# Routed rows added into three tables in memory, and the last shared products left in PSUM

## The chip, the cores and the metric

The kernel runs on one core of a Trainium2 chip. The metric is the device time of one execution in microseconds (us). All inputs and outputs are float32; the matrix products of the feed-forward part split each float32 operand into a high and a low part and sum three products.

## The reference, cut to what matters

```python
x = layernorm(x + attention(x))              # x: (2, 1024, 256), causal, 16 query heads, 4 key heads of 16
# feed-forward: one shared expert for every token, and 4 of 16 routed experts per token
scores = sigmoid(x @ gate_w.T) + gate_b
weights, indices = top_k(scores, 4);  weights /= weights.sum(-1)
shared = (silu(x @ w1_s) * (x @ w3_s)) @ w2_s                     # hidden width 176
routed = sum over the 4 chosen e of weights[e] * (silu((x @ w1[e]) * (x @ w3[e])) @ w2[e])
x = layernorm(x + shared + routed)
```

## The kernel before

The 2048 tokens are 16 tiles of 128 tokens. The span falls into three stages.

**Attention** (to about 310 us) follows one order written out by hand (`ORDER`, `plan`, `SEQ`), which every engine walks; an engine does its own part of each item. The DMA queue of SyncE (SP) walks it too: key and query parts, mask rows (`mrow`, one per group of heads, 16 of them) and weight loads. `padrow` is a row of zeros with a marker; SP writes it behind the expert regions of `xs_scratch`. At the end of each half of a batch the tokens are routed, and GpSimd (POOL) scatters each token's row, with its expert numbers, weights and four destinations, into the regions of its four experts (`scatter_rows`, 64 indirect DMAs).

**Feed-forward** runs 48 pairs of tiles (`NPAIR`): 4 shared pairs (`EARLY`, tiles 0 to 7), 40 routed pairs (`NRP`; the last of them, `LASTR` = pair 43, has one tile, so there are 79 routed tiles, `MOST`), then 4 shared pairs (44 to 47, tiles 8 to 15). Per pair TensorE (PE) turns the rows (`rows_back`), multiplies up into `psH` (`up`), turns the gated result (`gated_back`) and multiplies down into `psY` (`down`), interleaved over neighbouring pairs. A down product waits until `psY` of the pair before has been read. For a routed pair n (of 40), ScalarE (ACT) scales `psY` into `ys` (two buffers, `NYS`), and POOL scatters each tile of `ys` to `y4_scratch` (`send`, L839): every token has four rows of its own there, one per choice, so no two writes meet; rows of padding are out of bounds and dropped. For a shared pair VectorE (DVE) adds half of `psY` to the rows in `x1` (`scaled`, L1363). The last group of tokens is routed during the first pairs (`LATE`), and POOL's last eight row scatters stand one behind each of the first eight sends. SP loads the rows of routed pair n into `xs` three pairs ahead (L697 to L699).

**The end**: once the last up product is done and all sends have landed, SP reads `y4_scratch` back, four rows per token, 16 DMAs of 512 KB (L709). For each of the 16 tiles the four rows and the row of `x1` are summed: 8 tiles on PE (`token_rows`, L1739 and L1741: products with the identity into a PSUM bank, 5 rows of 256 columns), 6 on POOL (L854, L855, L858), 2 on DVE (L1371 to L1373); `ADDER` says who. Then come mean and variance on DVE (`statistics`), a square root on ACT (`deviation`), the reciprocal and shift on DVE (`shifts`), the scaling on ACT (`normalised`) and the output DMA (L713), in the units of `UNITS` and the order of `LAST_ORDER`.

Of the kernel before, what the change touches and what calls it, by code (L numbers as in the profile page):

```python
# [66 lines left out]
ADDER = (("pool", "dve"), ("pe", "pool"), ("pe", "pool"), ("pe", "pool"), ("pe", "pool"), ("pe", "pool"), ("pe", "dve"), ("pe", "pe"))  # L67
GATHER = [2, 1, 0] + list(range(3, NT))
SUMS = [(n, t) for n in range(NSHP) for t in range(2) if ADDER[n][t] == "pe"]
POOLED = [(n, t) for n in range(NSHP) for t in range(2) if ADDER[n][t] == "pool"]  # L70
UNITS = [((n, 0), (n, 1)) for n in range(NSHP - 1)] + [((NSHP - 1, t),) for t in range(2)]
LAST_ORDER = [("stat", 0), ("stat", 1), ("shift", 0), ("stat", 2), ("shift", 1), ("stat", 3), ("shift", 2), ("stat", 4), ("shift", 3),
              ("sum", 6, 1), ("shift", 4), ("stat", 5), ("stat", 6), ("shift", 5), ("stat", 7), ("shift", 6), ("shift", 7), ("stat", 8),
              ("shift", 8)]
FAR = B * T * TOPK
NXS, NYS, NSEL = 3, 2, 6
NSCAT = 8
PAD0 = 5
# [115 lines left out]
LASTU = [("wU", s) for s in range(10, NX)]  # L194

# [47 lines left out]
CONSTS, MASKS = 16, 10  # L243
# [10 lines left out]
def attention_moe(nc, x, wq_w, wq_b, wk_w, wk_b, wv_w, wv_b, cp_w, cp_b, gate_w, gate_b,  # L254
# [3 lines left out]
    y4_dram = nc.dram_tensor("y4_scratch", (FAR, C), F32, kind="Internal").ap()  # L258

    ctx = ExitStack()  # L260
    with ctx:
# [35 lines left out]
        j128 = sb("j128", [P, 1])  # L297
        lg = sb("lg", [P, TH, NE])
# [67 lines left out]
        y4 = sb("y4", [P, NT, TOPK, C])  # L366
# [120 lines left out]
        s_ysc = [sem(f"s_ysc{i}") for i in range(NYS)]  # L487
        s_y4a = [sem(f"s_y4a_{i}") for i in range(NSHP)]
        s_y4b = [sem(f"s_y4b_{i}") for i in range(NSHP)]
# [29 lines left out]
        def sum_bank(n, t):  # L519

            c = slice(0, C) if t else slice(C, 2 * C)
            if (n, t) == (NSHP - 1, 1):
                return psR[:, c]
            return (psR[:, c], psR2[:, c], psX[:, 1 - t, :, :].rearrange("p k t -> p (k t)"),
                    psG[:, 1 - t, :, :].rearrange("p k t -> p (k t)"), psH[:, 0, c], psH[:, 1, c], psY[:, 0, c], psY[:, 1, c])[n]
# [14 lines left out]
        def _(sp):  # L540
# [80 lines left out]
            def run(item):  # L621
# [24 lines left out]
                elif kind == "mrow":  # L646

                    k = item[1]
                    sp.wait_ge(s_Tfree, T_NO[item])
                    g = HEADGROUPS[k][2]  # L650
                    sp.dma_start(QS[ROWS:QROWS, QAT[(k // 2) % NSLOT], g % 2 * G:(g % 2 + 1) * G, :]
                                 .rearrange("s h (i t) -> s (h i) t", t=P), MT[:, :]).then_inc(s_mrow, 16)
                elif kind == "wload":
                    freed(item[1:])
                    load_weights(item[1:])

# [24 lines left out]
            for n in range(NRP):  # L681
# [23 lines left out]
            for i in range(NYS):  # L705
                sp.wait_ge(s_ysc[i], 16 * len([n for n in range(MOST) if n // 2 % NYS == i]))
            y4_rows = y4_dram.rearrange("(i p k) c -> p i (k c)", p=P, k=TOPK)
            for i in GATHER:
                sp.dma_start(y4[:, i, :, :].rearrange("p k c -> p (k c)"), y4_rows[:, i, :]).then_inc((s_y4a, s_y4b)[i % 2][i // 2], 16)  # L709
            for unit in UNITS:  # L710
                i0, i1 = 2 * unit[0][0] + unit[0][1], 2 * unit[-1][0] + unit[-1][1] + 1
                sp.wait_ge(s_norm2, i1)
# [5 lines left out]
        def _(pool):  # L718
# [30 lines left out]
            nc.gpsimd.iota(x1row[:, :, DT], pattern=[[P * TOPK, NT], [1, TOPK]], base=-FAR, channel_multiplier=TOPK,  # L749
# [82 lines left out]
            def send(n):  # L832

                pool.wait_ge(s_sel, n + 1)
                for t, s in enumerate((s_y0, s_y1)):
                    if 2 * n + t == MOST:
# [13 lines left out]
            def token_rows(n, t):  # L850

                i = 2 * n + t
                pool.wait_ge((s_y4a, s_y4b)[t][n], 16)
                link(nc.gpsimd.tensor_tensor(y4[:, i, 0:2, :], y4[:, i, 0:2, :], y4[:, i, 2:4, :], ALU.add))  # L854
                link(nc.gpsimd.tensor_tensor(y4[:, i, 0, :], y4[:, i, 0, :], y4[:, i, 1, :], ALU.add))  # L855
                if n >= EARLY:
                    pool.wait_ge((s_y0, s_y1)[t], n + NRP + 1)
                nc.gpsimd.tensor_tensor(x1[:, i, :], x1[:, i, :], y4[:, i, 0, :], ALU.add).then_inc(s_added, 1)  # L858

            pool.wait_ge(s_g, NPAIR)  # L860
            for n, t in POOLED:
# [4 lines left out]
        def _(act):  # L866
# [162 lines left out]
            def scaled(m):  # L1029
# [6 lines left out]
                if n >= NYS:  # L1036

                    act.wait_ge(s_ysc[n % NYS], 32 * (n // NYS))
# [34 lines left out]
            def normalised(u):  # L1073

                act.wait_ge(s_shift, u + 1)
                for n, t in UNITS[u]:
                    row = x1[:, 2 * n + t, :]
                    nc.scalar.activation(row, sum_bank(n, t) if (n, t) in SUMS else row, ACT.Identity, scale=rs2[:, n, t:t + 1],
                                         bias=sh2[:, n, t:t + 1]).then_inc(s_norm2, 1)

            act.wait_ge(s_const, CONSTS)
            for step in LAST_ORDER:
# [7 lines left out]
        def _(dve):  # L1090
# [217 lines left out]
            def product(m):  # L1308
# [4 lines left out]
                nc.vector.tensor_tensor(z[:, :, :], h1[:, :, :], psH[:, :, HID:2 * HID], ALU.mult).then_inc(s_z, 1)  # L1313
# [20 lines left out]
            def match(n):  # L1334
# [3 lines left out]
                if n >= NSEL:  # L1338
                    dve.wait_ge(s_y0, EARLY + n - NSEL + 1)
                    dve.wait_ge(s_y1, EARLY + n - NSEL + 1)  # L1340
                    dve.wait_ge(s_ysc[n % NYS], 32 * ((n - NSEL) // NYS + 1))
# [8 lines left out]
                nc.vector.tensor_scalar(dst[:, j, :], sel[:, j, :, 1], float(FAR), None, ALU.add).then_inc(s_sel, 1)  # L1350

            def scaled(m):

                if not shared(m):
# [3 lines left out]
                if n == 0 or n >= EARLY:  # L1358
                    for h in range(GROUPS - 1 if n == 0 else GROUPS):
# [6 lines left out]
            def token_rows(n, t):  # L1366

                i = 2 * n + t
                row = x1[:, i, :]
                dve.wait_ge((s_y4a, s_y4b)[t][n], 16)  # L1370
                link(nc.vector.tensor_tensor(y4[:, i, 0:2, :], y4[:, i, 0:2, :], y4[:, i, 2:4, :], ALU.add))  # L1371
                link(nc.vector.tensor_tensor(y4[:, i, 0, :], y4[:, i, 0, :], y4[:, i, 1, :], ALU.add))
                link(nc.vector.tensor_tensor(row, row, y4[:, i, 0, :], ALU.add))  # L1373

            for i in range(-2, NPAIR + 2):
                if 0 <= i < NPAIR:
                    gated(i)
                if i - 2 == NPAIR - 1:
                    token_rows(0, 1)
# [10 lines left out]
                for item in late(i, 0):  # L1390
                    run(item)
                if 0 <= i < NPAIR:
# [5 lines left out]

            def statistics(u):

                for n, t in UNITS[u]:
                    row = x1[:, 2 * n + t, :]
                    if ADDER[n][t] == "pe":
                        dve.wait_ge(s_sum, max(SUMS.index(u_) for u_ in SUMS if u_[0] == n and (n < NSHP - 1 or u_ == (n, t))) + 1)
# [410 lines left out]
```

## Time and profile before

| | us |
|---|---|
| median of 3 runs (547.24 to 548.96) | 547.45 |
| the profiled execution | 546.37 |
| its span, first to last instruction | 544.6 |
| PE busy | 519.8 (95%) |
| DVE busy | 431.9 (79%) |
| ACT busy | 372.5 (68%) |
| POOL busy | 290.4 (53%) |

Durations and starts below are from the one profiled execution and count from the start of its span; some 1.8 us of its time lie outside the span. Busy time of a DMA queue is not shown; a DMA has a time from issue to landing.

### The profile page before, as it was taken

What the parts mean: (1) busy time and instruction counts of PE and PEld (TensorE: products, weight loads), DVE (VectorE), ACT (ScalarE), POOL (GpSimd) and SP (SyncE); (2) the same over time, 40 slices, a digit from 0 to 9 for tenths busy, and PEclk for the clock granted to TensorE, in tenths of its full rate; (3) what the DMA queues carried; (4) which work ended last, traced back from release to release, by engine and by line L of the source; (5) the groups of instructions that cost most, each with busy time, mean ns of one, the idle gap of its engine ahead of it and who ended that gap; (6) DMA issues with size and microseconds to landing.
All of it is one profiled execution on the core that took longest, in us unless ns stands there. A gap on an engine that the chain in (4) does not pass through costs nothing.

```text
span 544.6 us, 12215 instructions
## 1 busy us (share of the span) xinstructions
PE 519.8 (95%) x3796; PEld 362.6 (67%) x3796; DVE 431.9 (79%) x1126; ACT 372.5 (68%) x841; POOL 290.4 (53%) x336
## 2 busy tenths in 40 slices
PE   7899999999999999989999998899999999999895
PEld 4555554644454555444433387799999999999874
DVE  2489998888889999979993178987788787887685
ACT  2357778577887788969699666466767676667544
POOL 5214243122674667476868755577654554545292
PEclk9999999999999999989999999999999999999999
DMA  5964760400041625620232351477544334341495
GB/s 151 181 72 63 171 196 1 90 0 21 1 82 62 112 72 144 169 99 22 89 124 69 105 176 38 135 243 237 171 129 137 114 119 122 110 126 46 164 416 193
DMA packets 53710, 64.96 MB, mean 119 GB/s; under 512 B 8091, under 2 KB 47406, under 8 KB 53648
## 3 DMA queue, kind: packets, MB, share of 16 engines
q1 hardware_dynamic: 45968, 46.45, 32.0%
q0 software_dynamic: 7056, 17.60, 9.2%
q8 instruction: 33, 0.54, 0.4%
q14 instruction: 29, 0.24, 0.2%
q10 hardware_dynamic: 624, 0.13, 0.1%
HBM read 32.49 MB, written 25.62 MB: 107 GB/s over the span
## 4 chain that ended last, share of the span: by engine, by line
PE 62%; DVE 20%; POOL 8%; issue 4%; ACT 3%; DMA 1%; SPq 1%; POOLq 0%; DVEq 0%; ACTq 0%
PE psH L1705 14%; DVE MX L1161 8%; PE psO L1491 8%; PE psS L1506 7%; PE psT L1476 7%; PE psS L1568 3%; PE psX L1673 3%; PE psG L1716 3%; POOL xs_scratch L766 2%; PE psS L1511 2%; PE psY L1729 2%; PE psY L1733 2%; PE psY L1730 2%; PE psY L1732 2%; PE psY L1731 2%
## 5 line engine op out<-in xcount | busy, mean ns | idle before, releaser
L885 ACT ACTIVATE prob<-psT 128x512 f32<-128x512 f32 (+3 forms) x384 | 166.5, 496 | 37.7 <-PE psT L1476 35.5
L1161 DVE TENSOR_REDUCE MX<-psS 128x1 f32<-128x512 f32 (+3 forms) x344 | 181.9, 594 | 9.4 <-PE psS L1506 4.6
L1506 PE MATMUL psS<-KS,QS 96*128 96x512 bf16 (+3 forms) x384 | 110.2, 329 | 3.6 <-DVE MX L1161 1.6
L839 POOL DMA_INDIRECT y_scratch<-ys,dst x79 | 77.1, 976 | 65.5 <-ACT ys L1040 50.6
L1476 PE MATMUL psT<-QS,KS 98*128 98x512 bf16 (+3 forms) x384 | 107.5, 327 | 1.0 <-ACT prob L885 0.6
L766 POOL DMA_INDIRECT xs_scratch<-x1row,slotu x64 | 64.6, 1010 | 39.7 <-DVE slotu L1243 24.5
L1705 PE MATMUL psH<-wU,xh 128*128 (+1 forms) x380 | 80.9, 334 | 0.5 <-DVE z L1313 0.4
L1491 PE MATMUL psO<-prob,V 128*32 128x512 f32 (+3 forms) x768 | 76.9, 496 | 3.4 <-POOL prob L795 3.2
L795 POOL TENSOR_SCALAR_AFFINE_SELECT prob<-prob 128x512 f32<-128x512 f32 x64 | 41.6, 652 | 62.7 <-ACT prob L885 62.4
L1476 PEld LDWEIGHTS psT<-QS,KS 98*128 98x128 bf16 x384 | 34.5, 98 | 48.7 <-ACT prob L885 26.7
L1705 PEld LDWEIGHTS psH<-wU,xh 128*128 128x128 f32 x380 | 61.8, 189 | 1.2 <-issue 1.1
L1506 PEld LDWEIGHTS psS<-KS,QS 96*128 96x128 bf16 x384 | 37.1, 98 | 36.0 <-DVE MX L1161 17.4
L1007 ACT COPY h<-psH 128x352 f32<-128x352 f32 x48 | 21.7, 453 | 52.7 <-PE psH L1705 52.7
L1305 DVE TENSOR_TENSOR xl<-psX,xh 128x512 fp32r<-128x512 f32 x48 | 33.1, 690 | 26.1 <-ACT xh L999 26.1
L1511 PE MATMUL psS<-mask_b,ident_b 128*128 128x128 bf16 x256 | 52.7, 220 | 0.0
L1705 PE MATMUL psH<-wU,xl 128*128 (+1 forms) x190 | 46.0, 323 | 0.0
L1491 PEld LDWEIGHTS psO<-prob,V 128*32 128x32 f32 x768 | 17.8, 108 | 33.2 <-issue 17.4
L1313 DVE TENSOR_TENSOR z<-h,psH 128x352 f32<-128x352 f32 x48 | 25.0, 521 | 11.6 <-ACT h L1007 11.3
L1511 PEld LDWEIGHTS psS<-mask_b,ident_b 128*128 128x128 bf16 x256 | 25.1, 98 | 13.6 <-issue 0.9
L1040 ACT ACTIVATE ys<-psY,sel 128x256 f32<-128x256 f32 x80 | 33.6, 471 | 0.3 <-PE psY L1733 0.3
L1331 DVE TENSOR_TENSOR gl<-psG,gh 128x512 fp32r<-128x512 f32 x48 | 33.1, 690 | 0.8 <-ACT gh L1027 0.7
L1705 PEld LDWEIGHTS psH<-wU,xl 128*128 128x128 f32 x190 | 33.4, 189 | 0.0
(260 smaller groups left out, 1001.5 us busy)
## 6 DMA issues: line engine op xcount, KB each, us to landing
xs<-xs_scratch SPq DMA_DIRECT2D x80, 134.0 KB
y<-y_scratch SPq DMA_DIRECT2D x16, 512.0 KB, 10.0
QS<-qp SPq DMA_DIRECT2D x48, 128.0 KB, 4.3
wU_raw<-in_L_ffn_w_routed_dram SPq DMA_DIRECT2D x32, 176.0 KB, 3.3
xs_scratch<-padrow SPq DMA_DIRECT2D x1, 2144.0 KB
xs_scratch<-padrow SPq DMA_DIRECT2D x16, 134.0 KB
x1row<-in_L_attn_x_dram SPq DMA_DIRECT2D x4, 512.0 KB, 5.6
out_dram<-x1row SPq DMA_DIRECT2D x7, 256.0 KB, 2.8
```

The lines of the kernel that those rows point to most:

```text
L766: nc.gpsimd.indirect_dma_start(xs_dram, bass.IndirectOffsetOnAxis(ap=slotu[:, h, i, k:k + 1], axis=0), x1row[:, tile_of(b, q * TH + i), :] ...
L795: nc.gpsimd.affine_select(out=blk, in_=blk, compare_op=ALU.is_ge, fill=0.0, base=0, pattern=[[0, G], [1, P]], channel_multiplier=-1).then_ ...
L839: nc.gpsimd.indirect_dma_start(y4_dram, bass.IndirectOffsetOnAxis(ap=dst[:, n % NSEL, t:t + 1], axis=0), ys[:, n % NYS, t, :], None, bound ...
L885: nc.scalar.activation(prob[:, step % NPROB, h, 0:HALF - c0], ps[:, 0:HALF - c0], ACT.Exp).then_inc(s_Tfree, 1)
L1040: nc.scalar.activation(ys[:, n % NYS, t, :], psY[:, t, 0:C], ACT.Identity, scale=sel[:, n % NSEL, t, 0:1]).then_inc(done, 1)
L1161: found = nc.vector.tensor_reduce(out=MX[:, c0 // HALF, heads[0]:heads[-1] + 1, i - TH * q], in_=src, op=ALU.max, axis=AX_X)
L1305: nc.vector.tensor_tensor(xl[:, m % 2, :, :, :], psX[:, :, :, :], xh[:, m % 2, :, :, :].bitcast(F32), ALU.subtract).then_inc(s_xl, 1)
L1476: mm(ps[:, 0:HALF - c0], KS[b][:, g, j * P:(j + 1) * P], QS[:, QAT[(k // 2) % NSLOT], g % 2 * G + h, c0:HALF], start=True, stop=True).then ...
L1491: last = mm(psO[32 * h:32 * h + 32, c0:HALF], V[b][:, j, g, :], prob[:, (PV_NO[item] - 1) % NPROB, h, 0:HALF - c0], start=(n == 0), stop=( ...
L1506: last = mm(ps[:, e * dist:e * dist + cols], QS[0:ROWS, QAT[(k // 2) % NSLOT], g % 2 * G + h, (i - TH * q) * P:(i - TH * q + 1) * P], KS[b ...
L1511: last = mm(ps[:, d:d + P], ident_b[:, :], mask_b[:, :], start=False, stop=True)
L1705: last = mm(psH[:, t, 0:2 * HID], a[:, m % 2, t, k, :], wU[:, e, n, k, :], start=((a, k, n) == parts[0]), stop=((a, k, n) == parts[-1]))
```

## The change

`y4_scratch` becomes `tab_scratch`: three tables of 2176 rows (17 blocks of 128; the first block is for padding), a token's three rows side by side. Routed tile j is **added** to table (j + 1) mod 3 by an indirect DMA with `compute_op=ALU.add`. Two adds to one table must not overlap, so add j waits until add j-3 has landed (`landed`). Padding rows no longer drop out: they go to row `jtab` of the padding block. Tables 1 and 2 and the padding block of table 0 are zeroed during attention (11 DMAs from `padrow`, one behind each of the mask rows 3 to 13). Table 0 starts as `x1`: tiles 8 to 11 are stored in the attention, tiles 12 to 15 at routed pair 3 of SP's loop, and tiles 0 to 7, with their shared product in them, at pairs 4 to 7; add 2, the first to table 0, waits for all six stores.

At the end three rows per token come back (384 KB per DMA), late tiles and early ones in turn. The down products of shared pairs 44 to 47 go to the PSUM banks of the sum and stay open; PE adds the three table rows of that tile there (`token_rows`), three such sums inside the pair loop and five behind it. The factor 0.5 moves into `product` for these pairs. The early tiles (0 to 7) are summed by POOL alone with two additions. `ADDER` and DVE's `token_rows` are gone; the first statistics moves into DVE's pair loop.

```diff
+NTAB = 3
+ROWS_EARLY = [(n, t) for n in range(EARLY) for t in range(2)]
+ROWS_LATE = [(n, t) for n in range(EARLY, NSHP) for t in range(2)]
+GATHER = [u for pair in zip(ROWS_LATE, ROWS_EARLY) for u in pair]
+UNITS = [((n, 0), (n, 1)) for pair in zip(range(EARLY, NSHP - 1), range(EARLY - 1)) for n in pair]
+UNITS += [((NSHP - 1, 0), (NSHP - 1, 1)), ((EARLY - 1, 0),), ((EARLY - 1, 1),)]
+LAST_ORDER = [("stat", 0)] + [step for u in range(1, len(UNITS)) for step in (("stat", u), ("shift", u - 1))]
+LAST_ORDER += [("shift", len(UNITS) - 1)]
...
+            return s_ysc[j % (2 * NTAB)], 16 * (j // (2 * NTAB) + 1)
...
@@ SP, attention @@
+                    if ZFIRST <= k < ZFIRST + len(ZEROED):
+                        zero_rows(*ZEROED[k - ZFIRST])
+                elif kind == "route":
+                    if b == B - 1:
+                        sp.wait_ge(s_x1, LN_NO[("ln", b, q * TH + TH - 1)])
+                        store_rows(tile_of(b, q * TH), TH)
...
@@ SP, routed pairs @@
+                if n == NXS:
+                    sp.wait_ge(s_x1, NT)
+                    store_rows(NT - TH, TH)
+                if NXS < n <= NXS + EARLY:
+                    pair = n - NXS - 1
+                    sp.wait_ge(s_y0, pair + 1)
+                    sp.wait_ge(s_y1, pair + 1)
+                    store_rows(2 * pair, 2)
...
-            for i in GATHER:
-                sp.dma_start(y4[:, i, :, :].rearrange("p k c -> p (k c)"), y4_rows[:, i, :]).then_inc((s_y4a, s_y4b)[i % 2][i // 2], 16)
+            for n, t in GATHER:
+                i = 2 * n + t
+                sp.dma_start(y3[:, i, :, :], tab_rows[:, 1 + i, :, :]).then_inc((s_y3a, s_y3b)[t][n], 16)
...
@@ POOL, send @@
+                    if j == 0:
+                        pool.wait_ge(s_zero, 16 * len(ZEROED))
+                    if j == 2:
+                        pool.wait_ge(s_xtab, 16 * (2 + EARLY))
+                    if j >= NTAB:
+                        pool.wait_ge(*landed(j - NTAB))
                     nc.gpsimd.indirect_dma_start(
-                        y4_dram, bass.IndirectOffsetOnAxis(ap=dst[:, n % NSEL, t:t + 1], axis=0),
-                        ys[:, n % NYS, t, :], None, bounds_check=FAR - 1, oob_is_err=False).then_inc(s_ysc[n % NYS], 16)
+                        tab_dram, bass.IndirectOffsetOnAxis(ap=dst[:, n % NSEL, t:t + 1], axis=0),
+                        ys[:, n % NYS, t, :], None, element_offset=(j + 1) % NTAB * C, bounds_check=NROW * NTAB - NTAB,
+                        oob_is_err=True, compute_op=ALU.add).then_inc(s_ysc[j % (2 * NTAB)], 16)
...
@@ POOL, early tiles @@
+                link(nc.gpsimd.tensor_tensor(y3[:, i, 0, :], y3[:, i, 0, :], y3[:, i, 1, :], ALU.add))
+                nc.gpsimd.tensor_tensor(x1[:, i, :], y3[:, i, 0, :], y3[:, i, 2, :], ALU.add).then_inc(s_added, 1)
...
@@ ACT, scaled @@
-                    act.wait_ge(s_ysc[n % NYS], 32 * (n // NYS))
+                    for t in range(2):
+                        act.wait_ge(*landed(2 * (n - NYS) + t))
...
@@ PE @@
+                    to = sum_bank(shared_pair(m), t) if m > LASTR else psY[:, t, 0:C]
...
-                mm(sum_bank(n, t), ident[:, :], x1[:, 2 * n + t, :], start=True, stop=False)
-                for k in range(TOPK):
-                    last = mm(sum_bank(n, t), ident[:, :], y4[:, 2 * n + t, k, :], start=False, stop=(k == TOPK - 1))
+                for k in range(NTAB):
+                    last = mm(sum_bank(n, t), ident[:, :], y3[:, 2 * n + t, k, :], start=False, stop=(k == NTAB - 1))
...
+                if i - 1 > LASTR + 1:
+                    token_rows(*ROWS_LATE[i - LASTR - 3])
                 if i - 1 == NPAIR - 1:
-                    token_rows(*SUMS[0])
+                    down(NPAIR - 2, (1,))
```

## Rows read from the trace of the kernel before

**Rows 1.** Windows: start:end, length, busy PE PEld DVE ACT POOL, PEclk, DMA share, GB/s
```profile
360.00:370.00 10.00, 10.00 (x78) 9.95 (x77) 8.26 (x24) 7.27 (x17) 7.56 (x9) 1.00 0.77 243
370.00:380.00 10.00, 10.00 (x76) 9.93 (x75) 7.67 (x24) 6.29 (x15) 7.87 (x8) 1.00 0.75 247
...
480.00:490.00 10.00, 10.00 (x79) 9.95 (x78) 8.30 (x24) 7.23 (x17) 4.87 (x5) 1.00 0.40 129
...
525.00:530.00 5.00, 5.00 (x25) 4.41 (x24) 4.05 (x17) 3.71 (x8) 4.76 (x6) 1.00 1.03 415
```
**Rows 2.** Timeline of PE at the end: start, us, instruction [idle before, releaser]
```profile
523.71 0.67 PE L1739 MATMUL psX<-x1row,ident 128*128 128x256 f32 x2 [1.23 <-DVE x1row L1363]
...
534.58 0.59 PE L1739 MATMUL psY<-x1row,ident 128*128 128x256 f32 x2
...
536.74 0.59 PE L1739 MATMUL psR<-x1row,ident 128*128 128x256 f32 x2
...
537.17 1.89 PE L1741 MATMUL psR<-y,ident 128*128 128x256 f32 x8
```
**Rows 3.** Timeline of DVE and ACT behind the last sum
```profile
539.62 0.42 DVE L1408 BATCH_NORM_STATS2 x1L<-psR 128x6 f32<-128x256 f32 x1
...
541.32 0.56 ACT L1078 ACTIVATE x1row<-psR,sh,rs 128x256 f32<-128x256 f32 x1 [0.42 <-DVE sh L1420]
```
**Rows 4.** Chain of waits, in order of time: start, us, what
```profile
528.37 0.73 POOL x1row L858
...
531.98 0.44 DVE x1L L1408
```
**Rows 5.** Line view of L709, the read back: ns min/median/max, first and last start
```profile
L709 SPq DMA_DIRECT2D y<-y_scratch x16: 332/447/1044, 510.0 to 518.0; - x16
...
DMA to landing us min/median/max: 3.5/10.0/16.4
```
**Rows 6.** Line view of L839, the sends
```profile
L839 POOL DMA_INDIRECT y_scratch<-ys,dst x79: 972/976/1026, 355.2 to 507.9; - x79
```
**Rows 7.** Timeline of POOL, sends of three successive pairs and the last
```profile
470.66 0.97 POOL L839 DMA_INDIRECT y_scratch<-ys,dst  x1 [1.75 <-ACT ys L1040]
...
471.94 0.98 POOL L839 DMA_INDIRECT y_scratch<-ys,dst  x1 [0.30 <-issue]
...
474.67 0.97 POOL L839 DMA_INDIRECT y_scratch<-ys,dst  x1 [1.75 <-ACT ys L1040]
...
507.85 0.98 POOL L839 DMA_INDIRECT y_scratch<-ys,dst  x1 [0.31 <-issue]
```
**Rows 8.** Line view of L766, the row scatters (137 KB each)
```profile
L766 POOL DMA_INDIRECT xs_scratch<-x1row,slotu x64: 969/988/1143, 169.1 to 385.6; - x64
...
DMA to landing us min/median/max: 2.4/2.5/4.9
```
**Rows 9.** DMA issues: out<-in, queue, count, KB each, median us to landing
```profile
x1row<-in_L_attn_x_dram SPq DMA_DIRECT2D x4, 512.0 KB, 5.6
out_dram<-x1row SPq DMA_DIRECT2D x7, 256.0 KB, 2.8
...
wA_raw<-in_L_ffn_w_shared_dram SPq DMA_DIRECT2D x1, 128.0 KB, 2.1
```
**Rows 10.** Timeline of the first sends: POOL, SP's loads for routed pair 7, ACT
```profile
359.06 0.98 POOL L839 DMA_INDIRECT y_scratch<-ys,dst  x1 [0.30 <-issue]
360.34 0.98 POOL L839 DMA_INDIRECT y_scratch<-ys,dst  x1 [0.30 <-issue]
...
356.91 0.89 SPq L699 DMA_DIRECT2D xs<-xs_scratch  x2
...
365.30 0.84 ACT L1040 ACTIVATE ys<-psY,sel 128x256 f32<-128x256 f32 x2
```
**Rows 11.** Line view of L855, POOL's 128x256 additions
```profile
L855 POOL TENSOR_TENSOR y<-y x6: 728/742/1127, 518.3 to 533.2; 128x256 f32<-128x256 f32 x6
```
**Rows 12.** Line view of L651, the mask rows to SBUF in the attention
```profile
L651 SPq DMA_DIRECT2D QS<-MT x16: 617/652/747, 32.7 to 288.3; - x16
```

More of the change, by code:

```diff
@@ L66 @@
 assert MOST == NTILE - 1
[L67 to L75, printed above, removed]
+NTAB = 3
[6 more added lines that the diff above has]
+LAST_ORDER += [("shift", len(UNITS) - 1)]
+NROW = P + B * T
 NXS, NYS, NSEL = 3, 2, 6
 NSCAT = 8
+ZCHUNK = 4
 PAD0 = 5
@@ L194 @@
 LASTU = [("wU", s) for s in range(10, NX)]
+ZEROED = [(k, m) for k in range(1, NTAB) for m in range(0, NROW // P, ZCHUNK)] + [(0, 0)]
+ZFIRST = 3
 def rows_steps():
@@ L1340, in match @@
                     dve.wait_ge(s_y1, EARLY + n - NSEL + 1)
-                    dve.wait_ge(s_ysc[n % NYS], 32 * ((n - NSEL) // NYS + 1))
+                    for t in range(2):
+                        dve.wait_ge(*landed(2 * (n - NSEL) + t))
                 for t in range(2):
@@ L1349, in match @@
                 link(nc.vector.tensor_reduce(out=sel[:, j, :, :], in_=prs[:, :, :, :], op=ALU.add, axis=AX_X))
-                nc.vector.tensor_scalar(dst[:, j, :], sel[:, j, :, 1], float(FAR), None, ALU.add).then_inc(s_sel, 1)
+                nc.vector.tensor_scalar(dst[:, j, :], sel[:, j, :, 1], jtab[:, 0:1], None, ALU.max).then_inc(s_sel, 1)
             def scaled(m):
-                if not shared(m):
+                if m >= EARLY:
                     return
@@ L1357, in scaled @@
                 n = shared_pair(m)
-                if n == 0 or n >= EARLY:
-                    for h in range(GROUPS - 1 if n == 0 else GROUPS):
+                if n == 0:
+                    for h in range(GROUPS - 1):
                         dve.wait_ge(s_scat[h], 16 * TH * TOPK)
@@ L1364, in scaled, with statistics @@
                                                    op0=ALU.mult, op1=ALU.add).then_inc(s, 1)
[L1366 to L1373, printed above, removed]
+            def statistics(u):
+                for n, t in UNITS[u]:
+                    if n >= EARLY:
+                        dve.wait_ge(s_sum, ROWS_LATE.index((n, t)) + 1)
+                        row = sum_bank(n, t)
+                    else:
+                        dve.wait_ge(s_added, ROWS_EARLY.index((n, t)) + 1)
+                        row = x1[:, 2 * n + t, :]
+                    last = nc.vector.bn_stats(st2[:, 2 * n + t, :], row)
+                link(last)
+                for n, t in UNITS[u]:
+                    last = nc.vector.bn_aggr(mv2[:, n, t, :], st2[:, 2 * n + t, :])
+                last.then_inc(s_var2, 1)
             for i in range(-2, NPAIR + 2):
@@ L1391, in _ @@
                     run(item)
+                if i == NPAIR - 1:
+                    statistics(0)
                 if 0 <= i < NPAIR:
@@ L1397, in _ @@
                     scaled(LASTR)
[L1399 to L1404, printed above, removed]
-                        row = sum_bank(n, t)
-                    elif ADDER[n][t] == "pool":
-                        dve.wait_ge(s_added, POOLED.index((n, t)) + 1)
-                    last = nc.vector.bn_stats(st2[:, 2 * n + t, :], row)
-                link(last)
-                for n, t in UNITS[u]:
-                    last = nc.vector.bn_aggr(mv2[:, n, t, :], st2[:, 2 * n + t, :])
-                last.then_inc(s_var2, 1)
             def shifts(u):
@@ L1717, in gated_back, with down @@
                 last.then_inc(s_gT, 1)
-            def down(m):
+            def down(m, which):
                 pe.wait_ge(s_gl, m + 1)
-                if m:
+                if 0 < m <= LASTR:
                     pe.wait_ge(s_y0, m)
@@ L1747, in _ @@
                 if i - 1 == LASTR:
-                    down(LASTR)
+                    down(LASTR, (0,))
                 if 0 <= i + 1 < NPAIR:
```

110 lines of the change are left out of this document (63 added, 47 removed).

## The prediction

> **What bounds the kernel now.** I read the windows first. In the routed stage PE is busy all the time, 10.00 of 10 us in slice after slice [rows 1]. POOL spends 0.98 us on each send and then idles 1.75 us once per pair [rows 6, 7], and DMA is busy 0.40 of the time (0.77 while the last row scatters still run) [rows 1]. So in this stage PE sets the pace, one pair per 4.0 us (474.67 - 470.66) [rows 7], and nothing that the change does to ACT, DVE or POOL there can save time; it can only cost some. The change adds nothing to PE there.
>
> The end is another matter. The read back is issued from 510.0 and lands up to 16.4 us after an issue [rows 5], so the last of it is there at about 518.0 + 16.4 = 534.4; the DMA engines are full then, 415 GB/s at a share of 1.03 [rows 1]. On PE a sum of five rows takes 536.74 - 534.58 = 2.16 us, and seven of them stand back to back from 523.71, when DVE has finished the last shared rows, to 537.17 + 1.89 = 539.06 [rows 2]. Behind the last sum come 2.8 us of statistics, root, shift and scaling (539.06 to 541.88) [rows 3] and 2.7 us of output until 544.6. The chain of waits goes through POOL's sums and DVE instead [rows 4]: three lanes (PE, POOL, transfers) end within a few us of each other. A gain needs all three to shrink, and all three do: PE and POOL have less to add, and the transfers carry a quarter less.
>
> **The end, worked out.** Call L the time from the start of an add on POOL to the moment when its landing is seen. For a plain send the last one starts at 507.85 [rows 7] and the read back at 510.0 [rows 5]: L = 2.16. No row shows an add. It reads its destination before it writes; a load of 128 KB from memory lands in 2.1 us [rows 9]. If the two were fully in series L would be 4.3; the lower end is 2.16. I take the middle, L = 3.2, so the read back starts at 507.85 + 3.2 = 511.05, 1.0 us later than before.
>
> The rule that weighs on this term is in the Trainium skill, "DMA: Bandwidth & Descriptors", section "Latency and other measured facts": an access to HBM costs 0.2 us on average and 2 us under high load. By it L would be 2.4 to 4.2 and the read back would start between 510.2 and 512.0; no row here shows it for an add, and my two bounds from rows are about the same.
>
> First landing: 3.5 us after the issue for 512 KB [rows 5], so 3.2 for 384 KB. The other 15 follow at the rate of the full DMA engines: 393 KB / 415 GB/s = 0.95 us each, 14.2 us. Output of the first four units (256 KB each, 1.05 MB) is issued before that ends and takes 2.5 us of the same engines. Last landing: 511.05 + 3.2 + 14.2 + 2.5 = 531.0. SP issues one DMA in some 0.45 us [rows 5], which is no limit.
>
> Against this rate speaks the same page of the Trainium skill, "DMA: Bandwidth & Descriptors", section "Measured (HBM→SBUF, 128 partitions, SWDGE, issued from GpSimd)": 341 GB/s for a transfer of 1 MB and less for smaller ones. By it the 6.3 MB would take 18.4 us and the end would come some 3.3 us later. The row of this kernel differs, 415 GB/s with transfers of 512 KB, and the row decides.
>
> PE: a sum is now three rows, 3/5 of 2.16 = 1.3 us, and needs no wait for DVE, since the shared product is in the bank already. Late tile number k is transfer 2k + 1; the last one (tile 15) lands second to last, at 530.0, and is summed by 531.3. PE's own work before that (three sums inside the loop, the last down products until about 522.7, then up to five sums of 1.3) ends at 529, so PE waits for data. The first sum stands in front of a down product and wants tile 8 at about 514.9; that lands at 514.3. If L is at its upper end PE waits 0.5 us there, and it idled about 1 us behind this place before.
>
> POOL: two additions per early tile at 0.73 [rows 11] plus hand-overs, 1.6 us; eight of them are 12.8 us, so POOL keeps up with one tile in 1.9 us and is last with the transfer: 531.0 + 1.6 = 532.6. Where DVE adds at the same time an addition takes up to 1.13 [rows 11]; DVE has no such additions any more. Then bn_stats to scaling: 0.4 + 0.2 + 0.3 + 0.2 + 0.2 + 0.6 and hand-overs, 2.0 us, and 0.5 because DVE and ACT still have the unit before: 535.1. Output 2.7: 537.8. Against 544.6 that is 6.8 us less.
>
> **The routed stage.** Add j waits for add j-3. With a pair every 4.0 us and 1.28 between the two of a pair [rows 7], the wait is free while L is below 4.0 + 1.28 = 5.28. Behind that wait on POOL stand only the next add and, in the first eight pairs, the row scatters. ACT reuses `ys` after two pairs and waits for the landing of an add that started 8.0 - 1.3 - 0.5 = 6.2 us before. At L = 3.2 both cost nothing; the cover is gone above 5.3.
>
> Add 2 is different: it waits for the store of tiles 6 and 7, which SP issues behind its loads for routed pair 7, at 356.91 + 0.89 = 357.8 [rows 10]. 256 KB land in 2.8 us, with a busy machine perhaps in 5.6 as 512 KB did [rows 9]: 360.6 to 363.4, where this send started at 359.06 [rows 10]. Add 3 then starts at 361.9 (364.7) and lands at 365.1 (up to 369.0); ACT needs it for the pair that it scales at 365.30 [rows 10]. So between 0 and 3.7 us on ACT, and in front of PE, which is full. POOL can't recover quickly there: three indirect DMAs of 1.28 fill 3.84 of 4.0 us. The stage also gets 1.6 MB of stores and the adds' reads at a DMA share of 0.77 [rows 1]. I take 0.5 us and keep 0 and 4. The loads of `xs` are three pairs ahead and cover themselves.
>
> The padding rows that are now written (79 x 128 - 8192 = 1920 of 1 KB, over the whole stage) are nothing at a share of 0.40.
>
> **The attention.** Eleven zeroing DMAs and one store stand in SP's queue. An issue costs up to 0.65 us of the queue [rows 12], and 4.6 MB cost the DMA engines 11 us at 415 GB/s. They follow a mask-row DMA, never precede it, and key and query parts are loaded ahead. Lower end 0, upper end 12 x 0.65 = 7.8 if each were on the path; I take 0.5, near the lower end since PE is full in nearly all of the attention too. The product with factor 0.5 has the same size as before and costs nothing.
>
> **Sum.** -6.8 + 0.5 + 0.5 = -5.8 us. The profiled execution took 546.37 (span 544.6 and 1.8 outside), so 540.6; the median of the runs shown is 1.1 higher, 547.45, which gives 541.6. With the terms at their good ends (L = 2.16, output not in the way) it is 537; with all at their bad ones, short of stalls by L, 547. That is this case's own range.
>
> **Rivals.**
> 1. *The adds land too slowly* (the other side). Three tables allow three adds in L + 0.3 us, so a pair takes 2 (L + 0.3) / 3. This passes 4.0 at L = 5.7. A row scatter without any add took up to 4.9 to land [rows 8]; with 2.1 for the read L = 7.0, a pair 4.87, and 38 pairs cost 33 us; with the read back 3.8 later the time is 578. For it: under load latencies of 4.9 are seen, and how fast a DMA engine adds is not in any row. Against: the median is 2.5 [rows 8], and the load is 0.40 in most of the stage. At L = 6.2 it is +13 and some 556.
> 2. *An add costs POOL more instructions than a copy.* Its send must exceed 2.0 - 0.3 = 1.7 us to decide; at twice 0.98 a pair takes 4.5, +19, 561. For it: the source and the destination are both read. Against: 0.97 to 1.03 for every indirect DMA, whichever its rows [rows 6, 8].
> 3. *Given back early:* the wait of add 2 and the stores cost their full 4, the zeroing 2: 541.6 + 5 = 546.6, no difference.
> 4. *More is won:* fewer bytes leave the DMA engines free, so the outputs cost nothing and L is short: 537 or a bit less.
>
> **Chances.** Forecast 0.62; rival 1 0.16, rival 2 0.05, rival 3 0.10, rival 4 0.07. A measurement can tell 0.3% (1.6 us) from no change. Faster: 0.58 of the forecast's, 0.05 of rival 3's and all of rival 4's, 0.70. Same: 0.03 + 0.05 = 0.08. Slower: 0.01 + 0.16 + 0.05 = 0.22. Range: 537 to 556, which leaves out the larger part of rivals 1 and 2 and the tip of rival 4.
>
> **What would show it.** A send on POOL near 0.98 us; pairs still 4.0 us apart at 470; POOL's idle time before sends still ended by ACT, not by a DMA; read back issued near 511; last additions of POOL at 532 to 533; PE sums of 1.3 us, the later ones with idle time in front. In the windows, DMA at 1.0 from 514 to 531. Wrong would be: sends waiting for DMA, ACT's `ys` waiting for one, pairs longer than 4.0, or a start of the routed stage that comes later than before (zeroing not hidden).

## The result: 1.7% slower, and the profile after

The changed kernel takes 557.94 us (median of 4 runs, 553.32 to 561.27) against 548.21 for the kernel before on the same chip: ratio 1.0171, 95% interval 1.0111 to 1.0230. I had forecast 541.6. The profiled execution is its shortest one, 553.32 with a span of 551.4, so 6.8 above the 544.6 of before; the three longer executions have a lower mean TensorE clock (0.988, 0.984 and 0.986 against 0.991). The traces can divide these 6.8 us, not the 9.7 between the medians. Ratios here and below leave out executions over 1.5% above their kernel's fastest, among them a few of 1283 to 2877 us in several kernels, the one before included; why they occur isn't known.

The page of the changed kernel; columns of the second block: line, engine, operation, count | busy us, mean ns | idle before, releaser.

```profile
span 551.4 us, 12221 instructions
PE 517.6 (94%) x3764; PEld 358.6 (65%) x3764; DVE 423.3 (77%) x1112; ACT 372.1 (67%) x841; POOL 329.3 (60%) x335
...
L888 POOL DMA_INDIRECT tab_scratch<-ys,dst x79 | 122.3, 1548 | 33.9 <-DMA tab_scratch<-ys,dst 15.7
...
L1087 ACT ACTIVATE ys<-psY,sel 128x256 f32<-128x256 f32 x80 | 33.5, 469 | 14.4 <-DMA tab_scratch<-ys,dst 14.4
```

A send takes POOL 1.55 us; before it was 0.98 [rows 6]. POOL now waits for earlier adds to land, and so does ACT with `ys`, which never stood still for a DMA before.

Line view of the sends of the changed kernel (ns min/median/max, first and last start), and its landing times:

```profile
L888 POOL DMA_INDIRECT tab_scratch<-ys,dst x79: 1535/1543/1774, 355.3 to 520.4; - x79
...
DMA to landing us min/median/max: 3.6/4.1/5.6
```

The timeline of POOL's last send and of SP's read back and outputs:

```profile
520.45 1.54 POOL L888 DMA_INDIRECT tab_scratch<-ys,dst  x1 [0.30 <-issue]
...
524.12 8.48 SPq L746 DMA_DIRECT2D y<-tab_scratch  x16
535.78 13.83 SPq L752 DMA_DIRECT2D out_dram<-x1row  x9
```

With this the 6.8 us split in three. The first send starts at 355.3, where it did before (355.2 in [rows 6]). The last starts at 520.45 instead of 507.85 [rows 7]: +12.6. From there to the read back 3.67 instead of 2.16: +1.5. From the read back to the end 551.4 - 524.1 = 27.3 instead of 544.6 - 510.0 = 34.6: -7.3. The sum is 6.8. So the end gives what I forecast, and the routed stage takes more than that away.

Where in the stage the 12.6 us arise is seen at send 16 (counted from 0), the first behind the eight pairs with row scatters. It starts at 397.97 in the changed kernel and at 387.06 in the kernel before, 10.9 us late already:

```profile
397.97 1.59 POOL L888 DMA_INDIRECT tab_scratch<-ys,dst  x1 [0.30 <-issue]
```
```profile
385.63 1.13 POOL L766 DMA_INDIRECT xs_scratch<-x1row,slotu  x1 [0.30 <-issue]
387.06 0.98 POOL L839 DMA_INDIRECT y_scratch<-ys,dst  x1 [0.30 <-issue]
```

Send 66 is 10.6 us late, and the last twelve add the other 2: at the end of the loop the sends of the kernel before come closer together (the last two 1.28 us apart, [rows 7] has the last) than adds can, 1.85 apart.

POOL's timeline in the first pairs of that stage; the windows behind it answer to [rows 1].

```profile
357.20 1.57 POOL L888 DMA_INDIRECT tab_scratch<-ys,dst  x1 [0.30 <-issue]
359.07 1.03 POOL L807 DMA_INDIRECT xs_scratch<-x1row,slotu  x1 [0.30 <-issue]
362.40 1.53 POOL L888 DMA_INDIRECT tab_scratch<-ys,dst  x1 [2.31 <-DMA tab_scratch<-x1row]
...
371.32 1.02 POOL L807 DMA_INDIRECT xs_scratch<-x1row,slotu  x1 [0.30 <-issue]
372.65 1.54 POOL L888 DMA_INDIRECT tab_scratch<-ys,dst  x1 [0.31 <-issue]
374.49 1.54 POOL L888 DMA_INDIRECT tab_scratch<-ys,dst  x1 [0.30 <-issue]
376.34 1.02 POOL L807 DMA_INDIRECT xs_scratch<-x1row,slotu  x1 [0.30 <-issue]
```

The windows (columns as there):

```profile
360.00:370.00 10.00, 8.18 (x62) 7.89 (x60) 5.21 (x15) 4.12 (x10) 6.47 (x6) 1.00 0.99 226
370.00:380.00 10.00, 9.00 (x48) 8.99 (x49) 6.24 (x18) 5.97 (x15) 8.16 (x7) 0.66 0.86 183
480.00:490.00 10.00, 10.00 (x75) 9.96 (x74) 7.86 (x23) 6.67 (x15) 7.54 (x6) 1.00 0.83 149
```

Read the releasers of the first fence: after add 2's one wait of 2.31 us (for the store of the last `x1` rows) there is only "issue", 0.30 us. A pair is one row scatter and two adds, 376.34 - 371.32 = 5.0 us, against PE's 4.0: POOL itself is the bound. The windows show what follows. PE stops for 1.8 us in the first of them and for 1.0 in the second, since ACT cannot reuse `ys`, and in the second its granted clock is 0.66 of the full one, with 48 matmuls instead of 76. The view of waits from 350 to 430 us names both links (us in total, times, longest):

```profile
ACT ys L1087 <- DMA tab_scratch<-ys,dst: 11.1, 8, 4.1
...
PE psY L1779 <- ACT ys L1087: 2.8, 1, 2.8
```

Later the picture is another one. From 400 to 411 us POOL sends every 1.85 us and catches up with ACT; from there it idles 0.5 us or more in front of most pairs, and from 420 us PE is full (10.00 of 10) at 4.0 us per pair. PE can't make good what it has lost. DMA is busy 0.83 of the time at 480 us instead of 0.40. That is the adding, for the same rows written plainly take 0.41 (experiment 1).

### The profile page after: what moved, and what is told of

The parts are those of the page before. It is cut to its first block, busy times and chain, and to the rows that moved or that the text cites. A ratio compares the mean times of both kernels' runs of the same rounds, so it can differ in the third digit from the quotient of the medians.

```text
span 551.4 us, 12221 instructions
## 1 busy us (share of the span) xinstructions
PE 517.6 (94%) x3764; PEld 358.6 (65%) x3764; DVE 423.3 (77%) x1112; ACT 372.1 (67%) x841; POOL 329.3 (60%) x335
## 4 chain that ended last, share of the span: by engine, by line
PE 44%; DVE 16%; DMA 15%; issue 8%; POOL 8%; ACT 4%; SPq 3%; POOLq 0%; ACTq 0%; DVEq 0%
DMA tab_scratch<-ys,dst 11%; PE psO L1531 8%; PE psS L1546 8%; PE psT L1516 8%; DVE MX L1209 6%; PE psH L1745 5%; POOL tab_scratch L888 4%; PE psS L1608 3%; DMA y<-tab_scratch 2%; PE psS L1551 2%; POOL xs_scratch L807 2%; PE psS L1618 1%; SPq L746 1%; PE psS L1632 1%; POOL prob L836 1%
## 5 line engine op out<-in xcount | busy, mean ns | idle before, releaser
L888 POOL DMA_INDIRECT tab_scratch<-ys,dst x79 | 122.3, 1548 | 33.9 <-DMA tab_scratch<-ys,dst 15.7
L1516 PEld LDWEIGHTS psT<-QS,KS 98*128 98x128 bf16 x384 | 34.5, 98 | 49.2 <-ACT prob L931 26.7
L1779 PE MATMUL psY<-wA,gh 128*128 (+1 forms) x89 | 29.3, 330 | 3.9 <-ACT ys L1087 3.3
```

The lines of the kernel that those rows point to most:

```text
L888: nc.gpsimd.indirect_dma_start(tab_dram, bass.IndirectOffsetOnAxis(ap=dst[:, n % NSEL, t:t + 1], axis=0), ys[:, n % NYS, t, :], None, elem ...
L1516: mm(ps[:, 0:HALF - c0], KS[b][:, g, j * P:(j + 1) * P], QS[:, QAT[(k // 2) % NSLOT], g % 2 * G + h, c0:HALF], start=True, stop=True).then ...
```

## The experiments

**1. Everything but the sum.** The changed kernel, its rows written over the tables' rows instead of being added. All waits, zeroing, stores and the end stay.

```diff
-    oob_is_err=True, compute_op=ALU.add).then_inc(...)
+    oob_is_err=True).then_inc(...)
```

> The changed kernel with plain writes in place of the adds; the tables, their zeroing, the stores of x1, every wait and the end stay as they are (so a token's rows overwrite each other and are not summed). Theory 1, POOL is the bound of the first eight routed pairs because it spends 1.54 us on an add against 0.98 on a plain send: sends are back at 0.98, the last send starts near 509 to 510 instead of 520.45, and the time is 540 to 543. Theory 2, the waits between tables, the zeroing and the stores are what costs: the sends get shorter but the last one still starts after 517 and the time stays above 550.

546.18 us (10 runs), ratio 0.9993 [0.9951, 1.0035], span 543.2. The sends came out as theory 1 has it, the time 3 us above its 540 to 543; experiment 5 returns to that. Its sends and its landing:

```profile
L888 POOL DMA_INDIRECT tab_scratch<-ys,dst x79: 969/973/1053, 356.7 to 509.8; - x79
...
DMA to landing us min/median/max: 2.4/2.4/3.9
```

The add alone costs some 10 us (0.0178 of 548): 0.57 us of POOL and 1.7 us of landing each. But it is two prices at once, and which of them counts is open.

**2. More `ys`, an earlier store.** If ACT's wait for `ys` and add 2's wait are what costs, a third and a fourth buffer and an earlier store bring it back. The first kernel has three buffers, the second stores the last early rows one pair earlier, the third has four buffers (the fourth lies over `x1L`) and ten `sel`/`dst`, the fourth all of this and the first two sends as plain writes.

```diff
-NXS, NYS, NSEL = 3, 2, 6
+NXS, NYS, NSEL = 3, 3, 6        # the third: 3, 4, 10
```
```diff
-    if NXS < n <= NXS + EARLY:
-        pair = n - NXS - 1
+    for pair in {NXS + 1: (0,), NXS + 2: (1,), NXS + 3: (2, 3)}.get(n, ()):
```

> The changed kernel with three ys buffers instead of two (r and rc of the attention lie over the third). Theory 1, POOL falls behind by about 1.0 us per pair while a row scatter stands in each (2 x 1.84 + 1.32 = 5.0 against 4.0) and ACT is stopped when two buffers are full: one more buffer absorbs one pair, 4.0 us, so the last send starts near 516.5 and the time is about 4 us below the changed kernel's. If instead the landing of adds over the tables (one table wait every third add) were the bound, a third buffer would give nothing, 0 to 1 us.

> The changed kernel with the last store of x1 (tiles 6 and 7) issued one routed pair earlier, at pair 6 of SP's loop beside tiles 4 and 5. Theory 1: add 2 waits 2.3 us for this store; it can start at 359.06 + 1.3 = 360.4 instead of 362.4, POOL's whole backlog shrinks by 2.0 us and the time by 2 us. Rival: the next bound (landing of add 3 before ACT may reuse ys) is reached anyway, because POOL has no slack in these pairs, and less than 0.5 us is won.

> The changed kernel with four ys buffers (the fourth lies over x1L) and ten sel/dst buffers instead of two and six, so that ACT and DVE are not stopped by POOL being behind. Theory 1 in its stricter form, POOL's own time is the bound of the whole routed stage: POOL never idles, and 79 x 1.85 + 8 x 1.32 + 2.3 us of store wait from 355.4 on put the start of the last send at 512 (changed kernel 520.4, before 507.9); the time is 8 us below the changed kernel's, 547 to 550, level with the kernel before. Rival: the landing of the adds (a table wait of 3.7 us every third add) is the bound, then the last send stays above 516 and less than 4 us is won.

> The same with two more reliefs of POOL: the last store of x1 one routed pair earlier, and the first send to table 1 and to table 2 as plain writes (their destination is zero, the sum is the same). Theory 1: 2.0 and 1.1 us less work and waiting on POOL, so the last send starts near 509 to 510, where PE's own pace of 4.0 us a pair ends; the three-row end then brings its 7 us less 2.1 us for the landing of the last add: 543 to 546, below the kernel before. Rival as for the run beside it: above 550.

Measured: 554.70 (ratio 1.0137 [1.0055, 1.0219]), 554.83 (1.0135 [1.0086, 1.0184]), 554.44 (1.0110 [1.0068, 1.0153]) and 552.67 (1.0098 [1.0061, 1.0134]). By the ratios they bring 1.9, 2.0, 3.3 and 4.0 us, where I expected 4, 2, 8 and 12 or more; each interval overlaps that of the changed kernel (1.0111 to 1.0230), so none of these gains is clear of the noise. The times and last sends of the last two (518.4 and 517.06) are those that I had set down for the rival, the landing of adds as the bound. The trace of the fourth doesn't bear that out: its sends waited for an earlier add four times, 0.30 us each, no longer than for an issue. Windows of the fourth kernel:

```profile
370.00:380.00 10.00, 10.00 (x76) 9.96 (x74) 7.83 (x23) 6.69 (x15) 8.17 (x7) 1.00 1.02 215
420.00:430.00 10.00, 10.00 (x79) 9.94 (x79) 8.17 (x25) 6.85 (x16) 8.32 (x6) 1.00 0.81 128
...
510.00:520.00 10.00, 6.15 (x42) 5.89 (x42) 5.39 (x12) 3.45 (x8) 7.39 (x5) 1.00 0.66 74
```

Its POOL timeline, and behind it that of DVE's `w`, which is made of two sources:

```profile
418.14 1.86 POOL L893 DMA_INDIRECT tab_scratch<-ys,dst  x1 [0.30 <-issue]
420.31 1.54 POOL L893 DMA_INDIRECT tab_scratch<-ys,dst  x1 [0.30 <-issue]
422.15 1.84 POOL L893 DMA_INDIRECT tab_scratch<-x1L,dst  x1 [0.31 <-issue]
...
483.71 1.54 POOL L893 DMA_INDIRECT tab_scratch<-ys,dst  x1 [1.83 <-ACT ys L1092]
...
487.41 1.54 POOL L893 DMA_INDIRECT tab_scratch<-x1L,dst  x1 [0.30 <-issue]
...
517.06 1.54 POOL L893 DMA_INDIRECT tab_scratch<-x1L,dst  x1 [0.30 <-issue]
```

```profile
418.06 0.53 DVE L1380 SCALAR_TENSOR_TENSOR w<-t,z 128x352 f32<-128x352 f32 x1
...
422.05 0.53 DVE L1380 SCALAR_TENSOR_TENSOR w<-t,z 128x352 f32<-128x352 f32 x1
```

PE now runs full at full clock to 500 us, and still the last send starts at 517.06, 9.2 us late; behind 510 it is PE that stands and waits for the read back. From 410 to 480 POOL never waits and never catches up: a pair costs it 1.54 + 1.86 and twice 0.30, 422.15 - 418.14 = 4.0 us, exactly PE's pace. So the delay that the first eight pairs leave, at 5.0 us each, stays (7.9 us at send 16, 7.5 at 478 us). At 482 us POOL stands 1.8 us for a `ys` that ACT fills late. From there no add is prolonged and a pair costs 487.41 - 483.71 = 3.7 us, which wins nothing any more, since the last pairs of the kernel before follow each other as fast. Buffers hide the delay from PE and bring back only PE's stops.

I had expected 3.7 us a pair all along. One add of two takes 0.3 us longer, and it is the one that starts just behind `w`. Set side by side, the POOL and DVE timelines of thirteen kernels (all but the first of experiment 4; 355 to 522 us) say the same. All 80 indirect DMAs, plain or adding, that start 0.05 to 0.25 us behind the start of the 352 wide `w` take longer than 0.98 or 1.54, by 0.14 to 0.36 us, and mostly the more the sooner they follow. The row scatter at 385.63 in the kernel before (1.13 us, `w` at 385.39) is one. Of the 270 during which `w` starts, none is longer by more than 0.06. This also explains the exact 4.0: a POOL that needs 3.7 us comes a little earlier in every pair until its first add stands just behind `w`, is held there, and from then on goes in step with PE and DVE (1.79 us at 410.21, then 1.81 to 1.86 in each pair). In the changed kernel all but two indirect DMAs fall elsewhere.

The Trainium skill, "SBUF — State Buffer", section "Who interferes with whom", says of the port that DVE and GpSimd share that a DVE instruction with two sources in SBUF holds off a GpSimd one that reads SBUF; it infers that the writing of DMA descriptors is spared by such a `tensor_tensor`. The traces agree with the first, if what is held off is the read of the row numbers `dst`, which lie in SBUF; whether it is that read or the writing of descriptors no run here separates, and I did not move `w`.

**3. The adds without the rest of the change.** The kernel before, its sends as adds on four zeroed rows per token: no tables, no waits of one add for another, no store.

```diff
+    sp.dma_start(<4 x 128 rows of y4_dram>, <zeros>)      # 16 of them, in the attention
...
-    ys[:, n % NYS, t, :], None, bounds_check=FAR - 1, oob_is_err=False)
+    ys[:, n % NYS, t, :], None, bounds_check=FAR - 1, oob_is_err=False, compute_op=ALU.add)
```

> The kernel before with its 79 sends turned into adds onto rows that are zeroed during the attention (16 DMAs of 512 KB, one behind each mask row); each token keeps four rows of its own, so there are no tables and no waits between adds, and the end is the old one. Theory 1: an add costs POOL 1.54 us here as well, the first eight pairs take 5.0 us each minus what the two ys buffers hide, the last send starts 6 to 9 us later than 507.85 and the time is 554 to 558. Theory 2, the waits between the tables: POOL's time per send alone does not matter, the time is 548 to 550. If the zeroing disturbs the attention, the first send starts later than 355.2.

557.75 us, ratio 1.0179 [1.0084, 1.0275], span 555.1; its sends take 1.54 us, its last one starts at 518.9, 11.1 us late (6 to 9 expected). So the order between adds (my rival 1 rests on it) isn't needed for the loss.

**4. POOL's time without any add.** One small POOL operation of 0.57 us ahead of each send, first in the copying kernel of experiment 1, then in the kernel before.

```diff
+    nc.gpsimd.tensor_tensor(spare[:, j:j + 1], eps_c[:, :], eps_pow[:, 0:1], ALU.pow)
     nc.gpsimd.indirect_dma_start(...)
```

> The copying version of the first experiment (rows are written in the three tables, not summed; transfers land after 2.4 us) with one small POOL operation of 0.59 us ahead of each send, so that a send takes POOL about 1.6 us, as an add does, while its transfer stays a plain write. The output holds no sums. Theory 'the time that an add takes on POOL is the cause': the backlog is as in the changed kernel, last send at 517 to 520, span 549 to 552, ratio 1.008 to 1.017. Theory 'the adds' reads and late landings are the cause': as the copying version, span 543 to 545, ratio 0.997 to 1.002. Half of each: 546 to 548.

> The kernel before with nothing changed but one small POOL operation of 0.57 us ahead of each send; its rows are still plain writes to four rows per token. Theory 'what an add costs is its time on POOL': this is as slow as the kernel before with adds in place of its writes (ratio 1.018), last send near 517 to 521, span 552 to 557, ratio 1.012 to 1.022, with transfers that still land in 2.4 us. Theory 'the reads and late landings of adds cost it': ratio below 1.005.

560.11 us, ratio 1.0203 [1.0149, 1.0256], and 558.64 us, ratio 1.0188 [1.0150, 1.0226]. The first lies above the 1.008 to 1.017 that I gave, the second within its range; the trace read is that of the second. POOL in the kernel before with the small operation:

```profile
372.20 0.97 POOL L768 DMA_INDIRECT xs_scratch<-x1row,slotu  x1 [0.30 <-issue]
373.19 0.58 POOL L841 TENSOR_TENSOR spare<-eps_c,eps_pow 128x1 f32<-128x1 f32 x1
373.96 1.03 POOL L842 DMA_INDIRECT y_scratch<-ys,dst  x1 [0.18 <-issue]
375.01 0.58 POOL L841 TENSOR_TENSOR spare<-eps_c,eps_pow 128x1 f32<-128x1 f32 x1
375.78 1.02 POOL L842 DMA_INDIRECT y_scratch<-ys,dst  x1 [0.18 <-issue]
377.11 0.98 POOL L768 DMA_INDIRECT xs_scratch<-x1row,slotu  x1 [0.30 <-issue]
...
515.57 1.03 POOL L842 DMA_INDIRECT y_scratch<-ys,dst  x1 [0.19 <-issue]
```

A pair takes 377.11 - 372.20 = 4.9 us, the last send starts 7.7 us late, and the time is that of experiment 3 (1.0188 beside 1.0179), with plain writes. This settles it: the time that a send takes on POOL is enough for the whole loss. Reading the destination, the later landing and the doubled share of the DMA engines are not needed for it. They may add their bit: in the profiled executions the adds of experiment 3 end 2.8 us later (555.1 against 552.3), of which 1.2 lie ahead of the first send, but the ratios show no difference.

**5. POOL's last instruction.** In experiment 1 the end didn't bring what it should: the last output has landed at 539.3, and the span ends at 543.2. In between stands a DRAIN with which POOL's program closes. The next kernel lets DVE add the last two early tiles of experiment 1, so that POOL is done earlier; the other does the same to the kernel with all buffers of experiment 2.

```diff
-    for n, t in ROWS_EARLY:          # POOL
+    for n, t in ROWS_EARLY[:-2]:     # the last two on DVE, ahead of their statistics
```

> The kernel with plain writes in place of the adds (rows overwrite each other, not summed), and the sums of the last two early tiles moved from POOL to DVE. Theory 3: the end of that kernel is not set by its work but by POOL's closing drain of 9.9 us, which starts with POOL's last addition at 533.0 and ends at 543.0, 3 us after the last output has landed; POOL then ends some 4 us earlier and the span falls from 543.2 to about 540, the time by 2.5 to 3 us. Rival: the drain just waits for the end of the program (it would be longer by what POOL ends earlier), or DVE's four extra additions stand on the path: no gain.

> The version with all reliefs of POOL in the routed stage and, besides, the last two early tiles summed by DVE. With adds the closing drain took 5.7 us instead of 9.9, so it hides behind the output; theory 3 then gives nothing here (within 1 us of the version without it). If DVE's additions (0.8 us each) stand on the path it is up to 2 us slower.

544.10 us, ratio 0.9933 [0.9896, 0.9969], and 551.59, ratio 1.0073 [1.0031, 1.0114]. The line views of that DRAIN (duration, start) and of SP's last one (when the outputs have landed): first the kernel before,

```profile
L261 POOLq DRAIN  x1: 9982/9982/9982, 534.4 to 534.4; - x1
L261 SPq DRAIN  x1: 7/7/7, 543.8 to 543.8; - x1
```

then the copying kernel of experiment 1, the one with DVE's two sums, and the changed kernel:

```profile
L264 POOLq DRAIN  x1: 9915/9915/9915, 533.0 to 533.0; - x1
L264 SPq DRAIN  x1: 7/7/7, 539.3 to 539.3; - x1
```
```profile
L264 POOLq DRAIN  x1: 9922/9922/9922, 528.1 to 528.1; - x1
L264 SPq DRAIN  x1: 7/7/7, 540.3 to 540.3; - x1
```
```profile
L264 POOLq DRAIN  x1: 5711/5711/5711, 545.0 to 545.0; - x1
L264 SPq DRAIN  x1: 7/7/7, 551.2 to 551.2; - x1
```

Behind plain indirect writes POOL's DRAIN takes 9.9 us, behind adds 5.7. It starts with POOL's last addition. Even the kernel before ends with it: 534.4 + 10.0 = 544.4, behind its outputs. Moving it took 2.6 us off the profiled span of the copying kernel (543.2 to 540.6) and 2.1 off the median, with intervals that overlap; where adds bind, the 0.0025 between the ratios (1.0098 and 1.0073) is within the noise. It does not explain the loss; it would have eaten a part of the gain.

**6. The other half of the change alone.** Plain writes to four rows per token as before, and only the end is the new one: late shared products stay in PSUM, and PE adds `x1` and four rows to each. POOL adds five early tiles, DVE three. The second kernel has another order at its end.

```diff
-    for k in range(NTAB):
-        last = mm(sum_bank(n, t), ident, y3[:, 2 * n + t, k, :], ...)
+    mm(sum_bank(n, t), ident, x1[:, 2 * n + t, :], ...)
+    for k in range(TOPK):
+        last = mm(sum_bank(n, t), ident, y4[:, 2 * n + t, k, :], ...)
```
```diff
+GATHER = GATHER[:12] + [GATHER[13], GATHER[12], GATHER[15], GATHER[14]]
-UNITS += [((7, 0), (7, 1)), ((3, 0),), ((3, 1),)]
+UNITS += [((3, 0),), ((3, 1),), ((7, 0),), ((7, 1),)]
```

> The second half of the change alone: rows are written as before (four per token, plain copies, 0.98 us of POOL each, 16 loads of 512 KB come back), and only the end is the changed one: late shared products stay in PSUM and PE adds five rows (x1 and four) to them; of the eight early tiles POOL adds five and DVE three. Theory (the loss is all in the adds' sends, the end is sound, and the 8.4 MB bound the end): last send near 508, read back near 510, last landing 534 to 536 as before, POOL's last sum before 532, so that its closing DRAIN of 9.9 us is no longer last; 544 to 548 us, ratio 0.995 to 1.000. If the PSUM end as such is worth the 7 us that I forecast for it, without its transfers having shrunk: 541 or less. Rival: PE's eight sums of 2.16 us behind the loop, or DVE's three, get on the path: 548 to 552.

> The kernel with the PSUM end alone, in another order at its end: the loads of the last two late tiles come behind those of the last two early ones, and DVE sums and closes the early tiles of pair 3 before it takes the statistics of the last late pair (in the trace of the former one it added them at 537.2 and 539.6, behind PE's last sum at 537.5). Theory (DVE's order held the end back): the last output is issued at some 539.5, span 542.5 to 544, ratio 0.993 to 0.998. If PE's last sum or POOL's closing DRAIN bound it in any case: no change, 1.000.

547.85 us, ratio 1.0006 [0.9969, 1.0042], and 548.88, ratio 1.0016 [0.9982, 1.0050]. No gain in either. The first kernel's chain of waits (start, us, what) ends in DVE's own sums:

```profile
537.18 0.61 DVE y L1383
...
538.74 0.44 DVE x1L L1386
539.63 0.61 DVE y L1383
```

The new order moved them ahead of the last late pair, and that brought nothing, against 0.993 to 0.998 expected. The profiled span fell from 545.4 to 543.8, but its routed stage starts 1.7 us earlier (first send at 353.5 against 355.2), and from the read back to the end it is 35.5 us against 35.4. With four rows to fetch and add per token the PSUM end is worth nothing: the kernel before takes 34.6 for the same stretch, the changed one 27.3. What differs between 35.4 and 27.3 is that three rows come back and not four, and those cost the adds.

## Why the prediction was wrong

**The step that failed** is the price of a send. I left it at 0.98 us ("0.97 to 1.03 for every indirect DMA, whichever its rows"). All the rows behind that sentence are plain writes; it was no evidence on an add. An add takes 1.54. That is my rival 2, and I gave it 0.05 because I set its threshold at 1.7 us per send, from two sends in 4.0 us. But in the paragraph on add 2 I had written that POOL's three indirect DMAs already fill 3.84 of 4.0 us in the first eight pairs. There the threshold is 2 (d + 0.3) + 1.28 = 4.0, d = 1.06, 0.08 above the price of before. With d = 1.54 a pair is 4.96 us, and eight pairs lose 7.7. Measured at send 16: 10.9 us in the changed kernel, 2 of them by add 2's wait, and 8.5 in experiment 3. Behind them 2 (1.54 + 0.3) = 3.7 lets POOL catch up with PE, and in the changed kernel it does, at 413 us. It doesn't help, for by then PE has lost the time itself.

**L** was taken too small, at little cost: the last one 3.67 us against 3.2 taken. Over the stage adds land after 4.1 (median; up to 5.6, above my upper end of 4.3), and 5.28 was the cover. POOL's 15.7 us in front of adds that waited for an earlier one are 26 times 0.30 of issue and 8 us beyond it, most of them behind 413 us, where PE is full and they cost nothing. The kernels of experiments 3 and 4 on the base of before have none of these waits and are as slow, so the waits are not needed for the loss. Rival 1 as I drew it, a pair of 4.9 us over 38 pairs, didn't come.

**Add 2's wait** was seen rightly: 2.31 us on POOL where I kept 0 to 4 and took 0.5. Too low is the 0.5 only because adds leave POOL no room to recover. With plain writes and the same wait the stretch from first to last send is 0.4 (experiment 1) and 1.5 us (experiment 5) longer than before. An earlier store brought 1 (profiled spans) to 3 us (medians), with intervals that overlap.

**Attention:** 0.1 us, 0.5 taken; but the first send of the kernels that share this attention starts anywhere from 354.2 to 356.8, so one trace doesn't size it. **The end:** right, in its steps too, as the profiled execution shows it. 27.3 us from read back to the end, 26.7 forecast; the last rows landed by 544.25, 20.1 us behind the first issue, against 19.95; a PE sum 1.46 to 1.6 where I had 1.3; POOL's last addition 545.05 + 0.72, 21.65 us behind the read back, against 532.6 - 511.05 = 21.55. In the medians this gain doesn't show: the changed kernel is at 1.0171, and the kernel before with adds and its old end (experiment 3) at 1.0179. The one runs at mean clocks of 0.984 to 0.991, the other at 0.997. Why, no run isolates. Not seen: POOL's DRAIN. With sends of 0.98 its last addition would have started at 532.6 + 1.0 (my two terms of 0.5) - 0.7 = 532.9 and the span ended at 532.9 + 9.9 = 542.8, not at 538.8 (540.6 less the 1.8 outside); experiment 1 measured 543.2. The copying kernel with DVE's two sums has neither fault, and it comes nearer the forecast: 542.34 in its profiled execution, 540.6 forecast. Over all its runs it is at 0.9933, where the forecast was 541.6 / 547.45 = 0.9893, just outside the interval: of 5.8 us some 3.7 are there.

**Not seen either:** that a stop of PE costs twice. The stop of 2.8 us at 368 us falls into 10 us at a mean clock of 0.66, worth some 3 us more, and the runs of the changed kernel, which scatter by 8 us, are on the whole longer where their mean clock is lower.

## What to carry to other kernels

Ask of each engine how full it is in the fullest stretch, not over the stage: POOL idled 1.75 us per pair at 470 us, and in the first eight pairs it had 4.0 - 3.84 = 0.16 left, and that decided. An operation that no row shows (here an add in place of a write) gets both bounds for its time on the issuing engine too, and not only for its transfer. And before trusting a gain at the end, look at what each engine does after its last useful instruction.

## What the runs showed of the hardware

- An indirect DMA that adds takes POOL 1.54 us for 128 rows, a plain one 0.98; it lands after 4.1 us (median) instead of 2.4. The share of the DMA engines at 480 us is 0.83, with the same rows written plainly 0.41.
- POOL's closing DRAIN takes 9.9 us behind plain indirect writes and 5.7 behind adds, though the last of them has landed some 20 us before. Why, no run here tells.
- An indirect DMA that starts 0.05 to 0.25 us behind DVE's two-source `w` takes 0.14 to 0.36 us longer (80 of 80, plain ones too); where `w` starts during it, it doesn't (270 of 270 within 0.06). A POOL with time in hand is caught there and held at PE's pace of 4.0 us (410 to 480 us in the fourth kernel of experiment 2).
- After a stop of 2.8 us in a full stage PE's granted clock fell to 0.50, its lower level of 1.2 GHz, for about 6 us. The changed kernel's windows of 2 us:

```profile
368.00:370.00 2.00, 0.18 (x2) 0.00 (x0) 0.00 (x0) 0.08 (x1) 1.69 (x2) 1.00 1.11 309
370.00:372.00 2.00, 1.00 (x4) 1.01 (x5) 0.74 (x2) 2.00 (x5) 1.70 (x2) 0.58 0.86 112
372.00:374.00 2.00, 2.00 (x12) 2.00 (x11) 1.91 (x7) 0.86 (x4) 1.69 (x2) 0.50 0.56 124
...
376.00:378.00 2.00, 2.00 (x13) 1.98 (x12) 0.40 (x2) 0.29 (x1) 1.39 (x3) 0.72 1.02 200
```
